# The next graph's input rows are normalised on ScalarE instead of on VectorE

## The reference

```
n   = layernorm(x)                     # per row, no gain, no shift
x1  = x + gru(n, conv(n), A @ relu(n @ w_msg))   # A = exp(-distance) * adj
out = x1 + experts(layernorm(x1))      # 8 experts, the best 2 of each row
```

## Time and profile before

| | us |
|---|---|
| median of 3 runs | 627.28 (626.98 to 632.03) |
| the profiled execution | 626.93 |
| its span, first to last instruction | 625.1 |
| VectorE busy | 492.4 (79%) |
| ScalarE busy | 369.1 (59%) |
| GpSimd busy | 329.5 (53%) |

### The profile page before, as it was taken

The page is one execution under the profiler, slowest core; times in us unless marked ns, Lnnn a source line. Parts: engine busy times, 40 slices in busy tenths (PEclk is TensorE's granted clock), DMA queues, the critical chain, the costliest instruction groups (busy, mean ns, idle before and its releaser), DMA issues. The chain is left out here.

```text
span 625.1 us, 13104 instructions
## 1 busy us (share of the span) xinstructions
PE 597.2 (96%) x4054; PEld 529.2 (85%) x4054; DVE 492.4 (79%) x2028; ACT 369.1 (59%) x715; POOL 329.5 (53%) x249
## 2 busy tenths in 40 slices
PE   7999999999999999999999999999999998999991
PEld 6788778787989897979898989898988978999990
DVE  7969898897989897989888888989887856544430
ACT  5644646466757574848484848576676735555440
POOL 2000505224367464758676675767675654565775
PEclk9989999999999999999999999999999999999996
DMA  8619131335456995665747465757565775766863
GB/s 305 201 45 316 48 117 60 111 96 187 129 150 167 298 259 169 149 182 128 203 121 188 130 156 142 185 133 195 133 177 125 221 167 143 166 158 158 209 112 42
DMA packets 92004, 99.72 MB, mean 160 GB/s; under 512 B 7520, under 2 KB 70752, under 8 KB 91616
## 3 DMA queue, kind: packets, MB, share of 16 engines
q1 hardware_dynamic: 70208, 82.37, 42.8%
q0 software_dynamic: 21728, 16.53, 16.4%
HBM read 74.95 MB, written 30.39 MB: 169 GB/s over the span
## 5 line engine op out<-in xcount | busy, mean ns | idle before, releaser
L986 POOL DMA_INDIRECT out<-y_t,xt x88 | 147.5, 1676 | 111.7 <-DMA out<-y_t,xt 62.8
L1021 POOL DMA_INDIRECT routed<-row,at_u x112 | 119.4, 1066 | 141.9 <-DVE at_u L1227 109.6
L561 PE MATMUL C<-cv_h,w_hi 128*128 128x256 f32 (+1 forms) x432 | 129.3, 299 | 1.1 <-issue 0.8
L562 PE MATMUL C<-cv_l,w_hi 128*128 128x256 f32 (+1 forms) x432 | 124.2, 288 | 0.0
L563 PE MATMUL C<-cv_h,w_lo 128*128 128x256 f32 (+1 forms) x432 | 123.8, 287 | 0.0
L561 PEld LDWEIGHTS C<-cv_h,w_hi 128*128 128x128 f32 x432 | 82.2, 190 | 2.6 <-issue 1.1
L562 PEld LDWEIGHTS C<-cv_l,w_hi 128*128 128x128 f32 x432 | 82.4, 191 | 1.1
L563 PEld LDWEIGHTS C<-cv_h,w_lo 128*128 128x128 f32 x432 | 82.3, 190 | 0.7
L737 PE MATMUL G<-ex,msg_t 128*128 128x512 f32 x128 | 58.9, 603 | 0.3 <-ACT gh L920 0.3
L634 PE MATMUL Y<-w_t,ge 128*128 128x128 f32 x424 | 55.8, 274 | 0.0
L634 PEld LDWEIGHTS Y<-w_t,ge 128*128 128x128 f32 x424 | 51.8, 191 | 3.1 <-issue 2.6
(11 more groups left out here) (270 smaller groups left out, 1650.9 us busy)
## 6 DMA issues: line engine op xcount, KB each, us to landing
w_t<-w_all SPq DMA_DIRECT2D x63, 392.0 KB, 3.7
adj<-adj_t SPq DMA_DIRECT2D x16, 1024.0 KB, 5.9
xt<-routed SPq DMA_DIRECT2D x63, 144.0 KB, 2.4
wd<-w_all SPq DMA_DIRECT2D x11, 392.0 KB, 4.5
x_ln<-x SPq DMA_DIRECT2D x16, 256.0 KB
x_res<-x SPq DMA_DIRECT2D x16, 256.0 KB
out<-x SPq DMA_DIRECT2D x15, 256.0 KB, 4.5
w_all<-w_s SPq DMA_DIRECT2D x1, 3136.0 KB, 9.7
```

The costliest lines, as they stand in the source:

```text
L561: pe.matmul(psum, hi(w), rhs_h, start=start, stop=False)
L562: pe.matmul(psum, hi(w), rhs_l, start=False, stop=False)
L986: nc.gpsimd.indirect_dma_start(out=out, out_offset=bass.IndirectOffsetOnAxis(ap=xt[j][:, t, R_ID:R_ID + 1].bitcast(U32), axis=0), in_=y_t[ ...
L1021: nc.gpsimd.indirect_dma_start(out=routed, out_offset=bass.IndirectOffsetOnAxis(ap=ats_u[d % 2][:, n:n + 1], axis=0), in_=rows[d % 2][:, n ...
```

## The change

VectorE's four tensor_scalar instructions of `normalize_x` go from the loop (those of graph 0, ahead of the loop, stay). In their place it computes `nbx` = -mean * rs, one small scalar_tensor_tensor of 128x4, and marks it with `nbx_done`. ScalarE writes `xl` with four activations of 128x128, x * rs + nbx, and gives `xl_ready`. They stand behind the four of `normalized_rows` and ahead of the copy to `xnT`.

```diff
--- before.py
+++ after.py
@@ -225,6 +225,7 @@
         rt_h = sb("rt_h", [P, 2 * NT])
         rt_t = sb("rt_t", [P, 2 * NT])
         nb = sb("nb", [P, NT])
+        nbx = sb("nbx", [P, NT])
         xl = sb("xl", [P, NT, P])
         xlT = sb("xlT", [P, NODES])
         xlT_h = sb("xlT_h", [P, NODES], F32R)
@@ -346,7 +347,7 @@
         diff_f32, diff_hi, diff_split = map(sem, ("diff_f32", "diff_hi", "diff_split"))
         nmp_split, gate_step, gru_step, xc_base = map(sem, ("nmp_split", "gate_step", "gru_step", "xc_base"))
 
-        root_step = sem("root_step")
+        root_step, nbx_done = sem("root_step"), sem("nbx_done")
         tab_step, xd_hi, xd_split = map(sem, ("tab_step", "xd_hi", "xd_split"))
         wd_in = [sem(f"wd_in{i}") for i in range(DENSE_BUFFERS)]
         xt_in = [sem(f"xt_in{i}") for i in range(RING)]
@@ -849,6 +850,13 @@
                                                 bias=nb[:, t:t + 1])
                 last.then_inc(xn_ready, 1)
 
+            def normalized_x(graph):
+                act.wait_ge(nbx_done, graph)
+                for t in range(NT):
+                    last = nc.scalar.activation(xl[:, t, :], x_ln[:, t, :], ACT.Identity, scale=rs[:, NT + t:NT + t + 1],
+                                                bias=nbx[:, t:t + 1])
+                last.then_inc(xl_ready, 1)
+
             def gap_weights(d):
                 act.wait_ge(rt_step, router_first(d) + ROUTER_GAP)
                 nc.scalar.activation(gap_t[:], gap[:], ACT.Tanh, scale=0.5).then_inc(gap_tanh, 1)
@@ -913,6 +921,8 @@
                 tile_turned(2)
                 if tail:
                     normalized_rows(d)
+                if more:
+                    normalized_x(g + 1)
                 if tail:
                     act.wait_ge(pe_xnT, d + 1)
                     nc.scalar.copy(xnT[:], G0[:]).then_inc(xnT_f32, 1)
@@ -1436,9 +1446,10 @@
                     all_roots(g, 0 if tail else NT, 2 * NT if more else NT)
                 if tail:
                     shift(d)
+                if more:
+                    nc.vector.scalar_tensor_tensor(out=nbx[:], in0=mv[:, 1, :, 0], scalar=-1.0, in1=rs[:, NT:2 * NT],
+                                                   op0=ALU.mult, op1=ALU.mult).then_inc(nbx_done, 1)
                 tile_weigh(0)
-                if more:
-                    normalize_x(g + 1)
                 dve.wait_ge(adj_loaded, 16 * g + 16)
                 for j in range(NT):
                     dve.wait_ge(exp_done, NT * g + j + 1)
```

## The result

| | before | changed |
|---|---|---|
| median of the runs timed side by side | 627.49 us (4 runs) | 637.64 us (4 runs, 635.6 to 639.11) |
| the profiled execution | 626.93 | 635.6 |
| its span | 625.1 | 633.8 |

The ratio is 1.0158, with a 95% interval of 1.0106 to 1.0209: 10 us slower. The forecast was 631.3 with a range to 636.5; the sign was right, the size too small by more than half.

The account below looks back on a forecast made before the run. TensorE, busy 597.2 of 625.1 us, was taken as the bound. Terms 3.5 + 0.5 + 0.2 = 4.2 us over the profiled 626.93 gave 631.1, stated as 631.3 for the median; range 627.0 to 636.5.

Parts of the forecast that it names:

- The bound: Whole span: TensorE bounds the kernel, busy 597.2 of 625.1 us, its longest sum of waits 2.7 us.
- VectorE's 16.6 us of relief: Loop on VectorE: 16.6 us of busy time removed, 2.2 us of small instructions added; costed at nothing gained.
- ScalarE's activations: Behind `row` on ScalarE: four more activations, 493 ns each; `xnT` later, a matmul wait of 0 to 0.1 us, swallowed later.
- The rule against `add` and `mul` on ScalarE: Skill page's rule for ScalarE's activations: a loss of at most 9.2 us; the forecast kept this term at zero.
- The load's landing: Load of x_ln, from issue to data seen landed: 2.8 us taken, between bounds of 2.4 and 5.0.
- Iterations 1 to 4: Late x_ln delays VectorE's statistics, so TensorE waits on `cv_l`: 0.5 us in iteration 1, 3.5 in iterations 2 to 4.
- Iterations 5 to 13: Statistics 1.4 us late in iteration 10, hidden by 1.8 us to spare up to `cv_l`; 0.2 us added for chances.
- Clearly slower: Rival: late load felt at `cv_l` in every expert iteration too; 633.6 to 640.5 us, chance 0.2.
- Not slower: Rival: the load of x_ln is hidden anyway, TensorE's spare time holds; 626.3 to 628.5 us, chance 0.13.
- The clock: Rival: clock halves in the new waits, up to 1.6 us each, four times 6.4, 637.5 us; chance 0.07.
- The stretch of iteration 1: Iteration 1, cited for the clock rival: granted clock 0.50 for 3.2 us, behind sixteen matmuls of one column.

Follow-up runs that it names:

- e1: Changed kernel with two buffers for x_ln, so its load goes out early again; 628.75 us against 628.95 before, ratio 1.0003.
- e5: Kernel before, with the load of x_ln made late (it also waits for a_prod) in iterations 0 to 4 alone; ratio 1.0068.
- f2: Changed kernel with two buffers for x_ln, load late (waits for ScalarE's xl) in iterations 0 to 4, early from 5 on; ratio 1.0070.
- f1: Changed kernel with two buffers for x_ln, load early in iterations 0 to 4, late (waits for ScalarE's xl) from 5 on; ratio 1.0053.
- e8: Changed kernel timed and profiled again with no edit; 638.49 us against 629.21 before, ratio 1.0146.
- e4: Changed kernel with VectorE's statistics of x_ln moved behind choose(), the load as late as in the changed kernel; 636.01 us, ratio 1.0092.
- e6: Kernel before, with the load of x_ln made late (it also waits for a_prod) from iteration 5 on alone; 628.82 us, ratio 0.9992.
- f3: As e1, but from iteration 5 on the load of adj, with x_res behind it, waits for ScalarE's xl; ratio 0.9964.
- f4: Kernel before, run and profiled again with no edit; one run, 628.71 us.
- e7: Changed kernel with VectorE's statistics of x_ln moved behind cv_l; 637.28 us, ratio 1.0116.

## Why the prediction was wrong

**The bound.** Right: TensorE, with no wait that the change could remove. VectorE's 16.6 us of relief brought nothing in any run, e1 included.

**ScalarE's activations.** Right: 1.64 us per four, 488 ns each, as `row`; they end 3.20 us after `row` starts, 3.22 forecast. `xnT` starts 3.10 us after `row` instead of 2.52, and the matmul behind it started at most some 0.1 us late, as forecast. The rule against `add` and `mul` on ScalarE (the Trainium skill, "ScalarE: Activation LUTs", "Rules for kernel authors") gave up to 9.2 us; e1 shows zero.

**The load's landing.** 2.8 us assumed, 2.95 in iteration 3 and 3.10 in iteration 10 of the changed profile (statistics less issue). The bounds held, the choice was near.

**Iterations 1 to 4.** Right: 0.5 + 3.5 = 4.0 us forecast; 3.85 from iteration 1's cast to iteration 5's in the first profile, 4.0 in the second, 4.3 and 4.4 as times in e5 and f2. One thing differs: TensorE waited mostly ahead of `pre`'s products, 0.81 to 0.91 us in the first profile, and lost 0.25 us more behind them ahead of `cv_l`'s matmul (iteration 3: 0.36 against 0.11). Together that is the 1.16 us that the prediction put on `cv_l` alone.

**Iterations 5 to 13.** This step failed. It read one chain, from `x_ln` to `cv_l`, found 1.8 us to spare and put the part at 0.2 us, and it put iteration 14 at nothing because no `x_ln` is loaded there. The chain did hold (0.57 us to spare in iteration 10). What went unread was GpSimd's list, in which 62.8 us of waits for earlier adds stood in the trace of before: a list paced by those landings, whose scatters release SyncE's `xt` loads. With the late `x_ln` load on top of ScalarE's `xl`, the first `xt` load slipped back by 2 to 3 us, until TensorE waited 2.5 to 3.0 us for it in iteration 14. The term was 3.3 us (f1 against the kernel before) where 0.2 stood. That the late load makes it is shown (f1 against e1, 1.0053 against 1.0003); that the longer GpSimd instructions under `ex` carry the other half is supported by their place and length, and not by a run of its own.

**The rivals.** "Clearly slower" named the right part of the program, and the measured 637.6 lies in its range (633.6 to 640.5), but its mechanism was wrong: TensorE never waited for `cv_l` there. That the range fits is luck. "Not slower" is out. The clock did not fall behind waits of 0.9 us, as the rows had it; it fell behind those of 2.5 and 2.6 in iteration 14 (e8, f1, e4), a length of which I had none on the list. The stretch of iteration 1 was read wrongly too: sixteen is the number of matmuls inside it, and what stood ahead of it were 32 matmuls of one column (line 671, 39.72 to 43.35).

**What stays open.** The sum of the measured terms, 3.3 + 4.4 = 7.7 us, is below the 9.2 to 9.9 of the changed kernel; the intervals allow both equality and a remainder. Why the late `x_ln` load pushes GpSimd's list back by 1 to 2 us in e6, and late `adj` and `x_res` by 1 us in f3, was seen and not taken apart; in iteration 14 of e8 SyncE issued `adj`, 1024 KB, at 469.38, while the add was being issued for whose landing the list then waited, but no run parts the two. Whether 0.5 us more lateness alone would do in e6 what f1 shows is open too.

## What to carry to other kernels

When an instruction moves to another engine, list who waits for the mark it gives, and follow each of them to the end; here the work was free on its new engine, and the whole loss came from a buffer's reload that hung on the mark, curable with a second buffer. And where the list of an engine that issues transfers is paced by their landings, a chain has to be read through it too, even if no row of the engine that bounds the kernel names it: its slack was used up by two small delays, each of which cost nothing alone in e1 and e6. Work that is moved away from a wait should be checked for whether it filled a gap where it stood (e4).

## What the runs showed of the hardware

- GpSimd's indexed DMA instructions, 0.96 to 0.99 us for a scatter and 1.57 for an add, took up to 3.29 and 3.62 us where they started under VectorE's four products of two operands in on-chip memory (2.48 us): 142 of 159 ended a fixed 0.85 to 0.95 (scatter) or 1.45 to 1.57 us (add) after the products' end. In e1 it is as strong as in the changed kernel, with `xt` in time all the same:

```profile
457.87 2.83 POOL L1032 DMA_INDIRECT routed<-row,at_u  x1 [0.30 <-issue]
...
459.86 0.38 SPq L501 DMA_DIRECT2D adj<-adj_t  x1
...
469.83 0.40 SPq L457 DMA_DIRECT2D xt<-routed  x1
```

- The granted clock fell to half for 3.4 us behind eight of the eleven waits of TensorE of 1.9 us or more, after the first iterations, in all fourteen profiles. The three without a fall are of 1.92 us (f4), 2.11 and 3.02 us (e7). It fell behind no shorter wait, so not behind the 0.7 to 1.0 us of iterations 2 to 4. The half-clock stretch of iteration 1 differs from run to run, 0, 3.4 or 6.8 us, for the same kernel.
